# Sums of squares of two head pairs in one batch of four column groups, and the norms' rows issued ahead of the weight loads

## The chip, the cores and the metric

The kernel runs on one core of a Trainium2 chip. The metric is the device time of one execution in microseconds. A profile is one execution of the program, recorded by the hardware profiler.

## The reference, cut to what matters

Four streams of 512 tokens with 256 features go through three layers: a mixture-of-experts feed-forward layer, a state-space layer ("attn" in the names), and the feed-forward layer again. The change is in the state-space layer only:

```
xp, z = x @ Wx.T, x @ Wz.T                       # 512 features = 64 heads x 8
Bm, Cm = (x @ WB.T), (x @ WC.T)                  # each 64 heads x 128 states
Bm = Bm * rsqrt(mean(Bm*Bm, over 128) + 1e-6) * Bn_w + B_bias    # Cm likewise
theta = cumsum((x @ Wth.T) * dt)                 # 64 heads x 64 angles
Bm, Cm = rope(Bm, theta), rope(Cm, theta)
h_t = alpha_t h_(t-1) + beta_t B_(t-1) x_(t-1) + gamma_t B_t x_t;  y_t = C_t . h_t
out = (y * silu(z)) @ Wout.T
```

The norms matter here: for each token and head, the mean of the squares over 128 states of B and of C, then one over its root.

## The kernel before, in words

The state-space layer is done stream by stream: scans 0 to 3, about 1.1 to 2.9 ms into the span. Scans 0 and 1 are unrolled in the program, 2 and 3 are a loop. A scan begins with a preparation (steps dt, decays, values x, which live in all heads) and then runs over 32 pairs of heads. A pair's B and C are four tiles [128, 512]: rows are 2 heads x 64 even (or odd) states, columns are tokens; tiles 0 and 1 are B even and odd, 2 and 3 are C. Four pairs make an iteration of a hardware loop (first and last iteration apart), and each of them is a "turn", even or odd by its place j.

All orders are written out by hand, one function per engine (`turn_pe`, `turn_act`, `turn_pool`, `turn_dve`, `turn_sp`); semaphores tie them. Turn n works on several pairs at once:

- TensorE: the sums of squares of pair n+2 (`ss_pe`, L1220); the outputs y of pair n-2 (`Y_pe`, L1414 and L1416, which waits for the states that `K_dve2` leaves); the products B^T C of pair n-1 (`G_pe`, L1350, which waits for GpSimd's rotation of that pair); transposes (L1359); tiles 0 and 1 of pair n+3 (`A_pe`, whose matmuls all stand at the helper's line L64); the states of pair n-1 (L1390); tiles 2 and 3 of pair n+3; the angles of pair n+2 (`T_pe`, also L64).
- ScalarE evacuates each tile twice: scaled into `xbc` (L1229), squared into `sq4` (L1231). In odd turns it also takes the root of the sums (`R_act`, L1238, into `stdr`, a part of `decay_t`).
- VectorE: angles' scan (`T_dve1`, L1171, waits for `T_pe`), decay scan (L1280), B^T C times the decay (`K_dve1`, L1374, waits for `G_pe`), y out of PSUM in odd turns (L1428, L1432), both norms multiplied in (`F_dve1`, L1274), in odd turns the reciprocal of the next norms (`R_dve`, L1250), four products with sine and cosine (`F_dve3`, L1298), the scan of the states (`K_dve2`, L1399).
- GpSimd: adds the diagonal (L1323), builds it for the next pair (L1318), and adds the products to rotated B and C (`F_pool`, L1306 and L1307); in scans 2 and 3 it also scatters tokens.
- SyncE issues the loads: broadcasts of per-head rows (L1149), angle weights (`th_load_sp`, L1055), the 1 MB of B and C weights for pair n+4 (`wb_load_sp`, L1047), and the norms' way.

The squares of a pair are summed over the partitions by a matmul with a [128, 32] one-hot matrix. f32 matmuls are two passes each, so the four matmuls of a pair are eight instructions in the trace. B goes to partitions 0 to 31 of the bank `SSB` (column group 0 of the array), C to 32 to 63 (group 1); even and odd states accumulate, and so do the two pairs of a couple, each in rows of its own. `sq4` is one buffer: a square of pair m waits for the sums of pair m-1.

After the odd pair of a couple the norms travel: root (`R_act`) -> `R_rows` copies 8 rows x 512 into 128 partitions x 32 (`rc_in`, 16 KB) -> reciprocal (`R_dve`) -> `R_sp2` writes them to memory (L1255) -> `R_sp3` reads them back, broadcast over partitions (`rr_bc`, L1264, 2 x 512 KB). `F_dve1` of the next even turn needs them. In scan 0 `R_rows` is issued by ScalarE's queue, in scans 1 to 3 by SyncE's, behind that turn's loads of `th` and `wb`. Scan 0 also splits each weight into a high and a low part and stores them, which scans 1 to 3 read; ScalarE (L1075, L1089) and VectorE (L1079, L1093) do that.

Of the kernel before, what the change touches and what calls it, by code (L numbers as in the profile page):

```python
# [68 lines left out]
def build(nc, x_in, w_gu, w_down, w_router, w_att, w_x, w_z, w_dtl, w_dth, a_log, w_out, bias_in, norm_w_in,  # L69
          rank_in, ident_in, cst_in, out):  # L70
    with ExitStack() as ctx:
# [88 lines left out]
        rot = [sb(f"rot{i}", [P, 4, SEQ]) for i in range(2)]  # L160
        tmp = sb("tmp", [P, 4, SEQ])
        ths, nfr = (sb(n, [P, SEQ]) for n in ("ths", "nfr"))
        sq4 = sb("sq4", [P, 4, SEQ])
        btr = sb("btr", [P, 2, SEQ])
        x1 = sb("x1", [P, NH, TT, HP])
        rho = sb("rho", [P, NH, TT])
# [17 lines left out]
        neg_a = sb("neg_a", [NH, 1])  # L184
        bias = sb("bias", [P, NP, 4])
        norm_w = sb("norm_w", [P, 4])
        stdr = decay_t[0:36, :, :, :].rearrange("p k q a -> p (k q a)")
        NORM_ROWS = slice(28, 36)
        rc_in, rc = sb("rc_in", [P, 32]), sb("rc", [P, 32])

        dks = [xc[:, i, :] for i in range(2)]
# [15 lines left out]
        oml = tmp[:, 2, TT * NH:].rearrange("p (t n) -> p t n", t=TT)  # L207
        dlt = tmp[:, 3, 0:TT * NH].rearrange("p (t n) -> p t n", t=TT)
        coef = tmp[:, 3, TT * NH:].rearrange("p (t n) -> p t n", t=TT)
        silu_z = [sq4[:, f, :] for f in range(KI)]  # L210
        gated = rot[1]
        row_dram = nc.dram_tensor("row_dram", [NP, 2, ROWW], F32, kind="Internal").ap()
        rr_dram = [nc.dram_tensor(f"rr_dram{i}", [8, SEQ], F32, kind="Internal").ap() for i in range(2)]
# [984 lines left out]
        def A_pe(e, m, j, cnt, parts=range(4), of=by_turns):  # L1198
# [4 lines left out]
            for i in parts:  # L1203
# [4 lines left out]
                else:  # L1208
                    e.wait_ge(e_X.sem, e_X.at(4 * m + i - 1))
                split_matmul(e, of(i)[:, :], [(pair_w(wb[j % 2], i, k), xpair[k]) for k in range(KD)],  # L1210
                             True, True).then_inc(e_pj.sem, 1)

        def ss_pe(e, m, j):
            if j % 2 == 0:
                e.wait_ge(e_sr.sem, e_sr.at(m // 2 if isinstance(m, int) else m >> 1))
            e.wait_ge(e_X.sem, e_X.at(4 * (m + 1)))
            for eo in range(2):
                for ty in range(2):
                    first = 30 - 28 * (1 - ty) - 2 * (j % 2)
                    ins = e.matmul(SSB[32 * ty:32 * ty + 32, :], one_hot[:, first:first + 32], sq4[:, 2 * ty + eo, :],  # L1220
                                   start=j % 2 == 0 and eo == 0, stop=j % 2 == 1 and eo == 1, skip_group_check=True)
            ins.then_inc(e_ssm.sem, 1)

        def A_act(e, m, j, parts=range(4), of=by_turns):
            if parts[0] == 0:
                e.wait_ge(e_t.sem, e_t.at(2 * (m - 3)))
            for i in parts:
                e.wait_ge(e_pj.sem, e_pj.at(4 * m + i + 1))
                e.activation(xbc[j % 4][:, i, :], of(i)[:, :], ACT.Copy, scale=norm_w[:, i:i + 1])  # L1229
                e.wait_ge(e_ssm.sem, e_ssm.at(m))  # L1230
                e.activation(sq4[:, i, :], of(i)[:, :], ACT.Square).then_inc(e_X.sem, 1)  # L1231

        e_rc = ev("e_rc")

        def R_act(e, gm):
            e.wait_ge(e_ssm.sem, e_ssm.at(2 * (gm + 1)))
            e.wait_ge(a_r1.sem, a_r1.at(gm))
            e.activation(stdr, SSB[0:36, :], ACT.Sqrt, scale=1.0 / NS, bias=eps_nm[0:36, 0:1]).then_inc(e_sr.sem, 1)  # L1238

        def R_rows(e, gm):  # L1240
            e.wait_ge(e_sr.sem, e_sr.at(gm + 1))
            e.nop(nofuse=True)
            e.wait_ge(e_rc.sem, e_rc.at(gm))
            e.nop(nofuse=True)
            e.dma_start(rc_in[:, :], stdr[NORM_ROWS, :].rearrange("r (c w) -> r c w", w=32)).then_inc(a_r1.sem, 16)

        def R_dve(e, gm):
            e.wait_ge(a_r1.sem, a_r1.at(gm + 1))
            e.wait_ge(a_r2.sem, a_r2.at(gm))
            e.reciprocal(rc[:, :], rc_in[:, :]).then_inc(e_rc.sem, 1)  # L1250

# [317 lines left out]
        def turn_sp(e, b, it, first, last):  # L1569

            N, Q, NB = b * NP + it * UN, it * UN, NP // UN
            for j in range(UN):
                n, q, p, jp = N + j, Q + j, N + j - 1, (j - 1) % UN
                T, A, SS, RG, K = in_turn(j, first, last)
                gm = b * (NP // 2) + it * 2 + j // 2
                if is_first(b) and not last:
                    wb_load_sp(e, b, q + 4, j)
                if not (last and j >= 2):
                    e.wait_ge(e_tu.sem, e_tu.at(n + 1))
                    e.nop(nofuse=True)  # L1580
                    dt_sp(e, q + 2, j + 2)
                    e.wait_ge(e_H.sem, e_H.at(n - 1))
                    e.nop(nofuse=True)
                    end_sp(e, q + 2, j + 2)
                if not (last and j >= 1):
                    e.wait_ge(e_th.sem, e_th.at(n + 2))
                    e.nop(nofuse=True)
                    th_load_sp(e, b, q + 3, j + 1)
                if not last:
                    e.wait_ge(e_pj.sem, e_pj.at(4 * (n + 3)))  # L1590
                    e.nop(nofuse=True)
                    if not is_first(b):
                        wb_load_sp(e, b, q + 4, j)
                if RG and not is_first(b):
                    R_rows(e, gm + 1)
                if not (last and j >= 2):
                    e.wait_ge(e_D.sem, e_D.at(n + 1))
                    e.nop(nofuse=True)
                    al_sp(e, q + 2, j + 2)
                if RG:  # L1600
                    R_sp2(e, gm + 1, (j // 2 + 1) % 2)
                    R_sp3(e, gm + 1, (j // 2 + 1) % 2)
# [99 lines left out]
            ins.then_inc(e_z.sem, 1)  # L1702

        def z_act(e, b, f):
            e.wait_ge(e_ssm.sem, e_ssm.at((b + 1) * NP))
            e.wait_ge(e_z.sem, e_z.at(KI * b + f + 1))
            e.activation(silu_z[f], XBANK[1][:, :], ACT.Silu).then_inc(e_sz.sem, 1)

# [220 lines left out]
```

## Time and profile before

| | |
|---|---|
| median of 3 runs | 3395.3 us (3392.41 to 3405.55) |
| the profiled execution | 3382.4 us, span 3380.6 us |
| busy: TensorE matmul / weight load | 2799.0 / 2118.0 us (83% / 63%) |
| busy: VectorE / ScalarE / GpSimd | 2326.1 / 1816.0 / 1501.2 us (69% / 54% / 44%) |
| TensorE's granted clock, mean | 0.909 of 2.4 GHz |
| pairs of scan 0 / 1 / 2 / 3, about | 620 to 1140 / 1240 to 1700 / 1850 to 2310 / 2400 to 2860 us |

PE is the matmul side of TensorE and PEld its weight loads, which overlap; DVE is VectorE, ACT ScalarE, POOL GpSimd, SP SyncE; a trailing q is an engine's DMA queue. An idle time in brackets stands before the instruction, with what ended it. Names are those of the program, without buffer numbers, and a view a tile is part of may lend it another name: `stdr` appears as `decay_t`, `SSB` as `bank`.

### The profile page before, as it was taken

To read this page: it belongs to the slowest core of one execution; us is meant where nothing else is said; L and a number is where in the kernel's file an instruction comes from. 1 tells how busy PE (TensorE), PEld (TensorE's weight loads), DVE (VectorE), ACT (ScalarE), POOL (GpSimd) and SP (SyncE) were. 2 spreads that over 40 slices of the span, in tenths; PEclk is the share of its full clock that TensorE was granted. 3 is DMA by queue.
4 is the path that set the end of the run, shared out by engine and by line. 5 is a ranking of instruction groups with operands and counts; after the bars stand their busy time and mean duration, and the time that the engine had idled before them with its cause. 6 is when DMAs were issued, how large, how long until landed. Compare 5 with 4: busy or idle time off the path is not lost.

```text
span 3380.6 us, 83925 instructions
## 1 busy us (share of the span) xinstructions
PE 2799.0 (83%) x28752; PEld 2118.0 (63%) x28752; DVE 2326.1 (69%) x3926; ACT 1816.0 (54%) x3740; POOL 1501.2 (44%) x1354
## 2 busy tenths in 40 slices
PE   4229997789999789999977999998899998549990
PEld 3118885466666557777754677776577776438870
DVE  5205354789999479999855999994799997324364
ACT  1006654577777167666514777763677774126650
POOL 2470155344444344455500666662456665340256
PEclk7559998899999799999978999999999999669995
DMA  9737896556665255566404666652566662548893
GB/s 389 239 131 233 261 296 200 169 181 198 209 192 179 91 158 156 166 172 173 114 1 127 184 175 169 177 152 63 173 179 182 178 174 77 216 138 256 281 288 118
DMA packets 315367, 609.71 MB, mean 180 GB/s; under 512 B 59152, under 2 KB 163728, under 8 KB 314128
## 3 DMA queue, kind: packets, MB, share of 16 engines
q1 hardware_dynamic: 272352, 501.29, 49.3%
q0 software_dynamic: 24576, 67.14, 6.2%
q10 hardware_dynamic: 18224, 38.54, 3.0%
q8 instruction: 120, 1.97, 0.2%
q14 instruction: 95, 0.78, 0.1%
HBM read 446.25 MB, written 159.51 MB: 179 GB/s over the span
## 4 chain that ended last, share of the span: by engine, by line
PE 63%; DVE 8%; ACT 7%; issue 7%; another core or an unknown queue 6%; DMA 5%; POOL 2%; ACTq 1%; SPq 1%; DVEq 0%; POOLq 0%
PE bank L64 23%; PE bank L572 6%; PE bank L1220 6%; PE bank L1350 4%; PE bank L1414 3%; PE bank L1390 3%; PE bank L1416 3%; PE bank L563 2%; PE cs_sn L586 2%; ACT btr L1365 2%; PE bank L1359 2%; PE bank L586 2%; DMA xl<-xd 1%; ACT sq L1231 1%
## 5 line engine op out<-in xcount | busy, mean ns | idle before, releaser
L64 PE MATMUL bank<-xh,wb 128*128 128x512 f32 x2048 | 677.7, 412 | 71.4 <-ACT btr L1365 37.8
L64 PEld LDWEIGHTS bank<-xh,wb 128*128 128x128 f32 x2048 | 367.6, 189 | 188.6 <-ACT btr L1365 58.1
L1229 ACT ACTIVATE xbc<-bank,norm_w 128x512 f32<-128x512 f32 x512 | 350.7, 685 | 234.0 <-PE bank L64 227.5
L1306 POOL TENSOR_TENSOR rot<-rot,tmp 128x512 f32<-128x512 f32 x256 | 330.7, 1292 | 204.0 <-DVE tmp L1298 204.0
L64 PE MATMUL bank<-xl,wb 128*128 128x512 f32 x1024 | 406.6, 397 | 0.0
L572 PE MATMUL bank<-wgu,xgT 128*128 (+1 forms) x1536 | 327.2, 337 | 92.0 <-issue 71.9
L648 DVE TENSOR_TENSOR hh<-sg,bank 128x96 f32<-128x96 f32 x384 | 97.5, 254 | 408.7 <-ACT sg L622 212.8
L1318 POOL TENSOR_TENSOR sq<-cst,rho 128x512 f32<-128x512 f32 x128 | 133.6, 1044 | 494.7 <-DVE xbc L1274 275.1
L1307 POOL TENSOR_TENSOR rot<-rot,tmp 128x512 f32<-128x512 f32 x256 | 331.4, 1295 | 0.0
L1298 DVE SCALAR_TENSOR_TENSOR rot<-xbc,bias,cs_sn 128x1024 f32<-128x1024 f32 x256 | 325.4, 1271 | 8.6 <-DVE xbc L1274 6.8
L1298 DVE SCALAR_TENSOR_TENSOR tmp<-xbc,bias,cs_sn 128x1024 f32<-128x1024 f32 x256 | 326.1, 1274 | 0.0
L1323 POOL TENSOR_TENSOR xc<-xc,sq 128x512 f32<-128x512 f32 x128 | 163.4, 1276 | 358.0 <-DVE xwp L1285 354.6
L1274 DVE TENSOR_TENSOR xbc<-xbc,rr_bc 128x1024 f32<-128x1024 f32 x256 | 308.0, 1244 | 5.7 <-DMA rr_bc<-rr_dram 3.7
L572 PEld LDWEIGHTS bank<-wgu,xgT 128*128 128x128 f32 x1536 | 249.2, 196 | 97.3 <-issue 96.2
L1231 ACT ACTIVATE sq<-bank 128x512 f32<-128x512 f32 x512 | 303.8, 593 | 4.1 <-PE bank L1220 3.1
L1220 PE MATMUL bank<-sq,cst 128*32 128x512 f32 x1024 | 245.3, 600 | 31.8 <-ACT sq L1231 31.0
L1365 ACT ACTIVATE btr<-bank 128x512 f32<-128x512 f32 x256 | 140.3, 595 | 232.5 <-PE bank L1359 230.5
L1416 PE MATMUL bank<-st,rot 128*64 128x16 f32 x3584 | 243.5, 214 | 0.0
L1416 PEld LDWEIGHTS bank<-st,rot 128*64 128x64 f32 x3584 | 230.9, 144 | 0.0
L64 PEld LDWEIGHTS bank<-xl,wb 128*128 128x128 f32 x1024 | 193.7, 189 | 47.9
L1414 PEld LDWEIGHTS bank<-x1p,sq 128*64 128x64 f32 x2048 | 135.5, 143 | 134.8 <-issue 116.7
L616 ACT ACTIVATE xgT<-bank 128x256 f32<-128x256 f32 x384 | 145.8, 380 | 120.2 <-remote 44.2
(293 smaller groups left out, 5840.3 us busy)
## 6 DMA issues: line engine op xcount, KB each, us to landing
wb<-watt_dram SPq DMA_DIRECT2D x96, 1024.0 KB
rr_bc<-rr_dram SPq DMA_DIRECT2D x128, 512.0 KB, 6.5
yd<-ys SPq DMA_DIRECT2D x96, 512.0 KB
wd<-w_down SPq DMA_DIRECT2D x384, 96.0 KB
dt_bc<-row_dram SPq DMA_DIRECT2D x256, 128.0 KB
al_bc<-row_dram SPq DMA_DIRECT2D x256, 128.0 KB
watt_dram<-wb ACTq DMA_DIRECT2D x29, 1024.0 KB, 5.2
xd<-xg SPq DMA_DIRECT2D x12, 2048.0 KB, 23.8
```

The source lines that it names most:

```text
L64: ins = e.matmul(dst, a, m, start=start and c == 0, stop=stop and c == n - 1, skip_group_check=not (start and stop))
L572: ins = e.matmul(gub[n % 2][:, 0:NI2], xgT[n % 3][:, k, :], w, start=k == 0, stop=k == KD - 1)
L1220: ins = e.matmul(SSB[32 * ty:32 * ty + 32, :], one_hot[:, first:first + 32], sq4[:, 2 * ty + eo, :], start=j % 2 == 0 and eo == 0, stop=j ...
L1229: e.activation(xbc[j % 4][:, i, :], of(i)[:, :], ACT.Copy, scale=norm_w[:, i:i + 1])
L1231: e.activation(sq4[:, i, :], of(i)[:, :], ACT.Square).then_inc(e_X.sem, 1)
L1274: e.tensor_tensor(both, both, r.unsqueeze(1).to_broadcast([P, 2, SEQ]), ALU.mult).then_inc(dst.sem, 1)
L1298: ins = e.scalar_tensor_tensor(o[:, 2 * ty:2 * ty + 2, :], X[:, i, :].unsqueeze(1).to_broadcast([P, 2, SEQ]), bias_of(i), cs_sn[:, :, :], ...
L1306: e.tensor_tensor(R[:, 2 * ty, :], R[:, 2 * ty, :], tmp[:, 2 * ty + 1, :], ALU.subtract)
L1307: ins = e.tensor_tensor(R[:, 2 * ty + 1, :], R[:, 2 * ty + 1, :], tmp[:, 2 * ty, :], ALU.add)
L1365: e.activation(btr[:, eo, :], XBANK[x][:, :], ACT.Copy).then_inc(e_bt.sem, 1)
L1414: e.matmul(o, m1[:, (a * TT + t) * CL:(a * TT + t + 1) * CL], c4(x1p[j][:, :])[:, a * TT + t], start=True, stop=True)
L1416: ins = e.matmul(y[CL:P, k, w:w + PW].rearrange("p (a d) -> p a d", a=2), R[:, 2 + eo, CL * k:CL * k + CL], hist[:, eo, :, :, k], start=eo ...
```

## The change

The sums of squares of a couple are taken together in its odd turn. In even turns `ss_pe` only waits for the squares. In odd turns it issues eight matmuls (16 passes): for even, then odd states, one to each of four column groups: B of the even pair, B of the odd pair, C of the even pair, C of the odd pair, at partitions 0, 32, 64 and 96 of the bank. `sq4` becomes two buffers, one per parity. `stdr` becomes a tile of its own with 128 partitions, and `R_rows` two DMAs of 8 KB in place of one of 16 KB. In scans 1 to 3 `R_rows` moves ahead of the `th` and `wb` loads in SyncE's order. Counts of semaphores follow.

```diff
@@ -160,7 +160,8 @@
         rot = [sb(f"rot{i}", [P, 4, SEQ]) for i in range(2)]
         tmp = sb("tmp", [P, 4, SEQ])
         ths, nfr = (sb(n, [P, SEQ]) for n in ("ths", "nfr"))
-        sq4 = sb("sq4", [P, 4, SEQ])
+        sq4 = [sb(f"sq4_{i}", [P, 4, SEQ]) for i in range(2)]
+        stdr = sb("stdr", [P, SEQ])
         btr = sb("btr", [P, 2, SEQ])
         x1 = sb("x1", [P, NH, TT, HP])
         rho = sb("rho", [P, NH, TT])
@@ -184,8 +185,6 @@
         neg_a = sb("neg_a", [NH, 1])
         bias = sb("bias", [P, NP, 4])
         norm_w = sb("norm_w", [P, 4])
-        stdr = decay_t[0:36, :, :, :].rearrange("p k q a -> p (k q a)")
-        NORM_ROWS = slice(28, 36)
         rc_in, rc = sb("rc_in", [P, 32]), sb("rc", [P, 32])
 
         dks = [xc[:, i, :] for i in range(2)]
@@ -207,7 +206,7 @@
         oml = tmp[:, 2, TT * NH:].rearrange("p (t n) -> p t n", t=TT)
         dlt = tmp[:, 3, 0:TT * NH].rearrange("p (t n) -> p t n", t=TT)
         coef = tmp[:, 3, TT * NH:].rearrange("p (t n) -> p t n", t=TT)
-        silu_z = [sq4[:, f, :] for f in range(KI)]
+        silu_z = [sq4[0][:, f, :] for f in range(KI)]
         gated = rot[1]
         row_dram = nc.dram_tensor("row_dram", [NP, 2, ROWW], F32, kind="Internal").ap()
         rr_dram = [nc.dram_tensor(f"rr_dram{i}", [8, SEQ], F32, kind="Internal").ap() for i in range(2)]
@@ -1210,15 +1209,19 @@
                 split_matmul(e, of(i)[:, :], [(pair_w(wb[j % 2], i, k), xpair[k]) for k in range(KD)],
                              True, True).then_inc(e_pj.sem, 1)
 
+        half = lambda m: m // 2 if isinstance(m, int) else m >> 1
+
         def ss_pe(e, m, j):
+            e.wait_ge(e_X.sem, e_X.at(4 * (m + 1)))
             if j % 2 == 0:
-                e.wait_ge(e_sr.sem, e_sr.at(m // 2 if isinstance(m, int) else m >> 1))
-            e.wait_ge(e_X.sem, e_X.at(4 * (m + 1)))
+                e.nop(nofuse=True)
+                return
+            e.wait_ge(e_sr.sem, e_sr.at(half(m)))
             for eo in range(2):
-                for ty in range(2):
-                    first = 30 - 28 * (1 - ty) - 2 * (j % 2)
-                    ins = e.matmul(SSB[32 * ty:32 * ty + 32, :], one_hot[:, first:first + 32], sq4[:, 2 * ty + eo, :],
-                                   start=j % 2 == 0 and eo == 0, stop=j % 2 == 1 and eo == 1, skip_group_check=True)
+                for g in range(4):
+                    first = 30 * (g % 2)
+                    ins = e.matmul(SSB[32 * g:32 * g + 32, :], one_hot[:, first:first + 32], sq4[g % 2][:, 2 * (g // 2) + eo, :],
+                                   start=eo == 0, stop=eo == 1, skip_group_check=True)
             ins.then_inc(e_ssm.sem, 1)
 
         def A_act(e, m, j, parts=range(4), of=by_turns):
@@ -1227,25 +1230,26 @@
             for i in parts:
                 e.wait_ge(e_pj.sem, e_pj.at(4 * m + i + 1))
                 e.activation(xbc[j % 4][:, i, :], of(i)[:, :], ACT.Copy, scale=norm_w[:, i:i + 1])
-                e.wait_ge(e_ssm.sem, e_ssm.at(m))
-                e.activation(sq4[:, i, :], of(i)[:, :], ACT.Square).then_inc(e_X.sem, 1)
+                e.wait_ge(e_ssm.sem, e_ssm.at(half(m)))
+                e.activation(sq4[j % 2][:, i, :], of(i)[:, :], ACT.Square).then_inc(e_X.sem, 1)
 
         e_rc = ev("e_rc")
 
         def R_act(e, gm):
-            e.wait_ge(e_ssm.sem, e_ssm.at(2 * (gm + 1)))
-            e.wait_ge(a_r1.sem, a_r1.at(gm))
-            e.activation(stdr, SSB[0:36, :], ACT.Sqrt, scale=1.0 / NS, bias=eps_nm[0:36, 0:1]).then_inc(e_sr.sem, 1)
+            e.wait_ge(e_ssm.sem, e_ssm.at(gm + 1))
+            e.wait_ge(a_r1.sem, a_r1.at(2 * gm))
+            e.activation(stdr[:, :], SSB[:, :], ACT.Sqrt, scale=1.0 / NS, bias=eps_nm[:, 0:1]).then_inc(e_sr.sem, 1)
 
         def R_rows(e, gm):
             e.wait_ge(e_sr.sem, e_sr.at(gm + 1))
             e.nop(nofuse=True)
             e.wait_ge(e_rc.sem, e_rc.at(gm))
             e.nop(nofuse=True)
-            e.dma_start(rc_in[:, :], stdr[NORM_ROWS, :].rearrange("r (c w) -> r c w", w=32)).then_inc(a_r1.sem, 16)
+            for h in range(2):
+                e.dma_start(rc_in[CL * h:CL * h + CL, :], stdr[CL * h + 30:CL * h + 34, :].rearrange("r (c w) -> r c w", w=32)).then_inc(a_r1.sem, 16)
 
         def R_dve(e, gm):
-            e.wait_ge(a_r1.sem, a_r1.at(gm + 1))
+            e.wait_ge(a_r1.sem, a_r1.at(2 * (gm + 1)))
             e.wait_ge(a_r2.sem, a_r2.at(gm))
             e.reciprocal(rc[:, :], rc_in[:, :]).then_inc(e_rc.sem, 1)
 
@@ -1582,6 +1586,8 @@
                     e.wait_ge(e_H.sem, e_H.at(n - 1))
                     e.nop(nofuse=True)
                     end_sp(e, q + 2, j + 2)
+                if RG and not is_first(b):
+                    R_rows(e, gm + 1)
                 if not (last and j >= 1):
                     e.wait_ge(e_th.sem, e_th.at(n + 2))
                     e.nop(nofuse=True)
@@ -1591,8 +1597,6 @@
                     e.nop(nofuse=True)
                     if not is_first(b):
                         wb_load_sp(e, b, q + 4, j)
-                if RG and not is_first(b):
-                    R_rows(e, gm + 1)
                 if not (last and j >= 2):
                     e.wait_ge(e_D.sem, e_D.at(n + 1))
                     e.nop(nofuse=True)
@@ -1702,7 +1706,7 @@
             ins.then_inc(e_z.sem, 1)
 
         def z_act(e, b, f):
-            e.wait_ge(e_ssm.sem, e_ssm.at((b + 1) * NP))
+            e.wait_ge(e_ssm.sem, e_ssm.at((b + 1) * (NP // 2)))
             e.wait_ge(e_z.sem, e_z.at(KI * b + f + 1))
             e.activation(silu_z[f], XBANK[1][:, :], ACT.Silu).then_inc(e_sz.sem, 1)
 
```

## Rows read from the trace of the kernel before

**Rows 1.** The page: the span, and the costliest-groups row of the sums of squares.
```profile
span 3380.6 us, 83925 instructions
...
L1220 PE MATMUL bank<-sq,cst 128*32 128x512 f32 x1024 | 245.3, 600 | 31.8 <-ACT sq L1231 31.0
```
**Rows 2.** Busy time in one stretch of scan 1; columns: stretch, length, engines, PE clock, DMA.
```profile
1300.00:1600.00 300.00, 293.60 (x3819) 215.62 (x3817) 274.27 (x349) 210.40 (x375) 152.97 (x125) 1.00 0.60 165
```
**Rows 3.** The chain that ended last, two pairs of scan 1: start, us, what.
```profile
1452.39 1.84 PE bank L1220 x8
...
1455.97 1.09 PE bank L1350 x64
...
1466.84 1.84 PE bank L1220 x8
...
1470.42 1.09 PE bank L1350 x64
...
1481.37 1.84 PE bank L1220 x8
```
**Rows 4.** Timeline of VectorE, the same two pairs: start, us, instruction [idle before].
```profile
1452.56 0.70 DVE L1171 SCALAR_TENSOR_TENSOR bank<-bank,dt_bc 128x512 f32<-128x512 f32 x1 [1.07 <-PE bank L64]
...
1457.13 0.76 DVE L1374 TENSOR_TENSOR sq<-bank,xc 128x256 f32<-128x256 f32 x2 [0.52 <-PE bank L1350]
...
1465.21 1.28 DVE L1298 SCALAR_TENSOR_TENSOR tmp<-xbc,bias,cs_sn 128x1024 f32<-128x1024 f32 x1
...
1472.27 2.35 DVE L1274 TENSOR_TENSOR xbc<-xbc,rr_bc 128x1024 f32<-128x1024 f32 x2
...
1479.55 0.84 DVE L1399 TENSOR_TENSOR_SCAN st<-end_bc,bank 64x128 f32<-64x128 f32 x2
1481.54 0.70 DVE L1171 SCALAR_TENSOR_TENSOR bank<-bank,dt_bc 128x512 f32<-128x512 f32 x1 [1.15 <-PE bank L64]
```
**Rows 5.** Timeline of GpSimd: its last rotation of the odd turn's pair.
```profile
1467.94 1.27 POOL L1307 TENSOR_TENSOR rot<-rot,tmp 128x512 f32<-128x512 f32 x1
```
**Rows 6.** Timeline of SyncE's DMA queue, same turn: weight load, norm rows, their way back.
```profile
1454.04 0.57 SPq L1047 DMA_DIRECT2D wb<-watt_dram  x1
1457.36 0.69 SPq L1245 DMA_DIRECT2D rc_in<-decay_t  x1
...
1461.79 0.33 SPq L1255 DMA_DIRECT2D rr_dram<-rc  x1
1463.42 1.29 SPq L1264 DMA_DIRECT2D rr_bc<-rr_dram  x2
```
**Rows 7.** The waits of the whole span: waiter, releaser, us in total, times, longest.
```profile
DVE rc L1250 <- DMA rc_in<-decay_t: 23.3, 29, 1.9
```
**Rows 8.** Timeline of SyncE's DMA queue, an odd turn of scan 2: the weight load.
```profile
2094.77 0.57 SPq L1047 DMA_DIRECT2D wb<-watt_dram  x1
```
**Rows 9.** Timeline of VectorE in that turn: the reciprocal of the norm rows.
```profile
2103.07 0.35 DVE L1250 RECIPROCAL rc<-rc_in 128x32 f32<-128x32 f32 x1 [1.66 <-DMA rc_in<-decay_t]
```
**Rows 10.** DMA issues of 1300 to 1600 us: the last number is us to landing.
```profile
rr_bc<-rr_dram SPq DMA_DIRECT2D x20, 512.0 KB, 5.8
```
**Rows 11.** Timeline of VectorE in scan 0, two pairs.
```profile
899.41 0.70 DVE L1171 SCALAR_TENSOR_TENSOR bank<-bank,dt_bc 128x512 f32<-128x512 f32 x1 [1.10 <-PE bank L64]
...
904.85 0.74 DVE L1374 TENSOR_TENSOR sq<-bank,xc 128x256 f32<-128x256 f32 x2
...
928.63 0.84 DVE L1399 TENSOR_TENSOR_SCAN st<-end_bc,bank 64x128 f32<-64x128 f32 x2
930.48 0.70 DVE L1171 SCALAR_TENSOR_TENSOR bank<-bank,dt_bc 128x512 f32<-128x512 f32 x1 [1.01 <-PE bank L64]
```
**Rows 12.** Timeline of TensorE, the same two pairs of scan 0.
```profile
902.97 1.16 PE L1350 MATMUL bank<-rot 64*64 64x64 f32 x64
...
915.79 1.91 PE L1220 MATMUL bank<-sq,cst 128*32 128x512 f32 x8 [1.57 <-ACT sq L1231]
```
**Rows 13.** Timeline of ScalarE's DMA queue in scan 0: the norm rows' issue.
```profile
904.22 0.69 ACTq L1245 DMA_DIRECT2D rc_in<-decay_t  x1
```

## The prediction

> **What bounds the kernel now.** First the busy table by stretch. In scan 1 between 1300 and 1600 us TensorE is busy 293.60 of 300 us at full granted clock (2.4 GHz), VectorE 274.27, ScalarE 210.40, GpSimd 152.97 [rows 2]. TensorE is the bound, VectorE close behind. Then the chain of waits: over two pairs it runs through TensorE's own instructions, with ScalarE's evacuation of the transposes (0.6 us a turn) the only other engine on it. A couple of pairs, from one odd turn's sums of squares to the next, takes 1481.37 - 1452.39 = 28.98 us [rows 3]. The two blocks of sums stand on that chain with 1.84 us each. Last the timelines of VectorE and GpSimd, for what is late next. VectorE waits 1.15 us for the angles' matmuls at the start of an odd turn, 0.52 us for the B^T C products in the middle of it [rows 4], and in some odd turns for the norms' rows: 23.3 us in 29 waits, 1.9 us at most [rows 7].
>
> **Part 1, the even turn's sums go.** TensorE loses 1.84 us per couple [rows 3]. The wait for the squares stays and costs no more than now, as the next instruction but one (`Y_pe`) needs the state scan of the odd turn anyway.
>
> **Part 2, the odd turn's sums double.** 16 passes in four column groups in place of 8 in two. Of today's 8 passes each takes 600 ns [rows 1], yet the 8 take 1.84 us: two run abreast, 0.46 us a round. If four run abreast, 16 passes are again four rounds, 1.84 us; if only two, 3.7 us. Those are the bounds (nothing speaks for less than 1.84). The nearest row is L1350: 64 passes of 64 columns, an eighth of the columns, so 0.058 us a round; two abreast they would take 1.8 us, four abreast 0.93 us plus one pass's tail. They take 1.09 [rows 3]. Its tiles are two row halves by two column halves, and not four column groups, but four different streams do enter the array at once. I take 1.84 us.
>
> Against it stands a rule: the Trainium skill, "TensorE: Matmul & The Clock Gate", section "Part 3: Packing small matmuls — row/col tiling", measured three column groups of 32 at 2.38 times one, not 3. By that efficiency the block would take about 2.3 us, an estimate from that page, and each couple would lose 0.5 us of the gain worked out below; no row here has more than two column groups of 32 at work.
>
> **What is late next in scans 1 to 3.** If TensorE alone counted, a couple would take 27.1 us. But the even turn's G_pe (L1350, 1470.42) would then start at 1468.6, and it needs the rotated pair, whose last GpSimd operation ends at 1467.94 + 1.27 = 1469.21 [rows 5]. So G_pe moves up to about 1469.3 only. The ring that closes is: G_pe even to sums odd, 1481.37 - 1470.42 = 10.95; sums odd to G_pe odd, 1455.97 - 1452.39 = 3.58; to VectorE's product that waits for it, 1457.13 - 1455.97 = 1.16 [rows 3, 4]; from there to the end of its last rotation product, 1465.21 + 1.28 - 1457.13 = 9.36 [rows 4]; to the end of GpSimd's last addition, 1469.21 - 1466.49 = 2.72; and 0.1 to wake TensorE. Sum 27.87 us, 1.1 less than 28.98. VectorE by itself needs 1479.55 + 0.84 - 1452.56 = 27.83 with its waits for TensorE in it, 27.3 without the 0.52, so it fits under this ring.
>
> This ring holds only in turns in which the reciprocal does not wait for the norms' rows; today that wait hides behind TensorE, in the new ring it would stand on the path at its full size (23.3 us over 48 couples, 0.5 each).
>
> **Part 3, the rows go ahead of the weight load.** The rows are issued when the root is there (1457.36), after the loads of `th` and `wb` (1454.04) [rows 6]. They arrive behind the 1 MB: in the slowest turns 8.3 us after the weight load's issue (2094.77 to 2103.07, with 1.66 us of wait) [rows 8, 9]. Ahead of the loads they meet an empty queue, and the wait goes. That gives back the 0.5 us a couple.
>
> But something is queued behind them now. `th` and `wb` are held until the root is there. With the rows' second DMA (another 0.3 to 0.7 us of issue, from the 0.33 and 0.69 of rows 6) the weight load leaves some 2.2 us after the rows, at about 1459.6 instead of 1454.04. Its own user, the next turn's first projection, is at about 1472, so the load is in time. The reciprocals, however, are sent off at 1461.79 as today, and now it is they that stand behind 1 MB. Bounds: if they pass the weights, they land as today, at 1463.4 [rows 6]; if they wait as the rows do in the slowest turn, at 1459.6 + 8.3 + 0.5 (for the decay rows between them) = 1468.4. I take 6.6 us behind the weight load's issue, since the nearest transfer of the same size, the two halves of `rr_bc`, needs 0.65 + 5.8 = 6.5 [rows 6, 10]: 1466.7. Then `rr_bc` is issued and lands 6.5 us later, at 1473.2 (bounds 1469.9 and 1474.9). VectorE wants it at 1472.27 [rows 4].
>
> Is that 0.9 us on the path? In the new order VectorE has the 0.52 us wait before its product in the odd turn to swallow part of it. The ring through the norms spans two couples: sums odd to rows 5.0 (1452.39 to 1457.36), rows to `rr_bc` 15.8, even norm product to next angle scan 8.2 (1472.27 to 1480.47), angle scan to last rotation product 13.93 - 0.52 = 13.4, GpSimd and wake 2.8, G_pe to sums 10.95 [rows 3 to 6]. Sum 56.2, or 28.1 us a couple. It is longer than 27.87 by 0.25, and every further microsecond of landing costs 0.5. With the bounds of the landing a couple takes 27.9 to 28.95 us. I take 28.1: 0.88 us less than today. A scan has 15 even turns with sums (one more is in the preparation), so 3 x 15 x 0.88 = 39.6 us, less 2 for first and last turns: 38.
>
> The Trainium skill, "DMA: Bandwidth & Descriptors", section "Queues, rings and completion order", says that the descriptors of an issuing engine are taken in ring order on each DMA engine, but that completion is not first in, first out: a small transfer may finish on some rings early. If it let the 16 KB pass the weights, `rr_bc` would be in time and the sum 45 x 1.1 = 50 us for scans 1 to 3. The trace is against it: 16 KB wait for 1 MB today [rows 7].
>
> **Part 4, scan 0.** The order of DMAs stays. Two pairs take 930.48 - 899.41 = 31.07 us. VectorE is busy without a pause longer than 0.2 us from 899.41 to 928.63 + 0.84 = 929.47, then waits 1.01 [rows 11]; TensorE waits 1.57 us for squares before the even turn's sums [rows 12]. Without the sums G_pe of the even turn starts 1.84 us earlier, and VectorE's wait goes: 30.07 us a couple, 1.0 less, times 15 is 15 us. The second small DMA sits in ScalarE's queue there (0.69 us for the one now [rows 13]), just before the evacuation of the transposes; its 0.35 to 0.7 us fit into the 0.8 us by which TensorE is then ahead. If that cover were gone it would cost up to 0.7 x 15 = 10 us.
>
> **Part 5, at nothing.** The preparation loses one block of sums per scan and one wait of the squares; its steps run on VectorE and SyncE, so 0, at most 4 x 1.84 = 7 us gained. The root over 128 instead of 36 partitions, the buffers and the counts: 0.
>
> **Sum.** 38 + 15 = 53 us off the profiled execution's own 3382.4: 3329.4. The median of the runs stands 12.9 above that execution, so 3342.
>
> **Rivals.**
> A. The norms come late for good. If the reciprocals land 8.4 us or more behind the weight load's issue in place of 6.6, the ring is 28.98 and beyond: scans 1 to 3 gain nothing, and lose 45 x 0.5 = 22 us per further microsecond. For it: the load is held 5.5 us, and the longest wait today stands for 8.3 us; against it: in most turns the wait is far under that. At the edge 3395 - 15 = 3380; slower than before from 9.1 us on (the 15 us of scan 0 are then spent), and at 10.5 us about 3412. Chance 0.14, of which 0.04 ends slower.
> B. The four groups do not run abreast. The odd block takes 3.7 us, TensorE saves nothing, and the block stands in the ring of scans 1 to 3 (it lies between angles and G_pe, for which VectorE waits): 28.1 + 1.84 = 29.9, 0.95 more than today, 45 times 43 us. In scan 0 G_pe ends at 904.13 and VectorE comes at 904.85 [rows 11, 12], so 1.1 us of wait eat the gain there. 3395 + 43 = 3438. It decides from a block longer than about 2.8 us. Against it: L1350. Chance 0.07.
> C. All of it comes, and more: the norms in time, VectorE's slack found, a couple at 27.4 to 27.5 us, the preparation's share too: 45 x 1.55 + 15 + 5 = 90 us, 3305. VectorE's 27.3 allow it; the ring through GpSimd speaks against it. Chance 0.15.
> D. The move does nothing (the rows still wait 0.5 us): 28.4 us, 26 + 15 = 41 us, 3354; within the forecast's range.
>
> **How the numbers follow.** The forecast has 0.60, range 3325 to 3362; A 0.14, B 0.07, C 0.15, and 0.04 is for what I don't see. The overall range is 3308 to 3384. What a measurement of this kernel can tell is 0.5%, 17 us. Faster by more: forecast, C, and 0.05 of A: 0.80. Within: 0.09 of the rest of A and others: 0.11. Slower: B and the end of A: 0.09.
>
> **What would show it.** Right: L1220 only in odd turns, 16 passes in about 1.9 us; a couple in scans 1 to 3 at 27.9 to 28.3 us; no more wait of L1250 for `rc_in`; a wait of up to 1 us of L1274 (even turns) for `rr_bc`; TensorE waiting under 1 us before the even turn's outputs or L1350; scan 0 at 30.1 us with no wait of L1171. Wrong: a block of 2.5 us or more (B), waits of L1274 above 2 us (A), a granted clock below full in the middle of the scans, or a couple under 27.6 us (C).

## The result, and the profile after

The changed kernel takes 3500.91 us (median of 3, 3493.09 to 3506.56), the kernel before 3395.3. The ratio is 1.0301, 95% interval 1.0255 to 1.0348: 106 us slower, where 53 us faster had been forecast. The profiled execution has a span of 3491.3 us.

The page after has a new wait in the row of VectorE's norm product, 5.7 us in all before (3.7 of them for `rr_bc`). Columns as in [rows 1].

```profile
L1278 DVE TENSOR_TENSOR xbc<-xbc,rr_bc 128x1024 f32<-128x1024 f32 x256 | 306.0, 1237 | 159.3 <-DMA rr_bc<-rr_dram 140.3
```

VectorE now stands idle 140.3 us for `rr_bc` ahead of that product. The busy table by stretch (engines in the order PE, PEld, DVE, ACT, POOL, then granted clock, DMA share, GB/s): three pieces of one couple of scan 0, and 300 us of scan 1, which answers to [rows 2].

```profile
918.00:930.60 12.60, 9.56 (x86) 7.30 (x84) 12.29 (x18) 9.63 (x18) 7.02 (x6) 1.00 0.68 223
930.60:937.40 6.80, 6.80 (x107) 6.31 (x105) 5.59 (x9) 2.58 (x5) 1.27 (x1) 0.50 0.94 245
937.40:950.00 12.60, 12.37 (x169) 8.94 (x172) 10.45 (x12) 10.20 (x18) 6.10 (x5) 1.00 0.33 123
1350.00:1650.00 300.00, 273.69 (x3551) 212.78 (x3549) 256.20 (x330) 197.34 (x348) 142.15 (x117) 0.94 0.54 154
```

TensorE is no longer the bound (273.69 of 300 where it was 293.60), and the clock, which was granted in full in these pairs before, falls to 1.2 GHz at times, in scan 0 twelve times in twelve couples. The second row is such a fall. TensorE's timeline there: it waits for the squares of the even turn, and the outputs (`Y_pe`, 16 columns each) come right behind.

```profile
930.10 0.20 PE L1418 MATMUL bank<-x1p,sq 128*64 128x16 f32 x1 [2.08 <-ACT sq L1234]
```

The 64 passes of `G_pe` behind them took 1.99 us, where they had taken 1.16 in [rows 12].

A couple in scan 1, TensorE's timeline: the sums are in odd turns only, 16 passes in 1.92 us, as forecast. Eight passes over two groups had taken 1.91 us in such a timeline [rows 12], which the chain of [rows 3] has as 1.84.

```profile
1508.20 1.92 PE L1223 MATMUL bank<-sq,cst 128*32 128x512 f32 x16
```

VectorE over the same couple answers to [rows 4]: angle scan of the odd turn, the reciprocal, the even turn's norm product with its wait, and the next odd turn's angle scan.

```profile
1479.93 0.70 DVE L1170 SCALAR_TENSOR_TENSOR bank<-bank,dt_bc 128x512 f32<-128x512 f32 x1
...
1489.22 0.34 DVE L1254 RECIPROCAL rc<-rc_in 128x32 f32<-128x32 f32 x1
...
1503.31 2.36 DVE L1278 TENSOR_TENSOR xbc<-xbc,rr_bc 128x1024 f32<-128x1024 f32 x2 [3.03 <-DMA rr_bc<-rr_dram]
...
1511.47 0.70 DVE L1170 SCALAR_TENSOR_TENSOR bank<-bank,dt_bc 128x512 f32<-128x512 f32 x1
```

SyncE's queue answers to [rows 6]: rows, angle weights, the 1 MB, decay rows, reciprocals, `rr_bc`.

```profile
1484.73 1.29 SPq L1249 DMA_DIRECT2D rc_in<-stdr  x2
1486.35 0.62 SPq L1054 DMA_DIRECT2D th<-watt_dram  x1
1487.31 0.60 SPq L1046 DMA_DIRECT2D wb<-watt_dram  x1
1488.14 1.21 SPq L1148 DMA_DIRECT2D al_bc<-row_dram  x2
1489.63 1.20 SPq L1259 DMA_DIRECT2D rr_dram<-rc  x1
1495.92 1.29 SPq L1268 DMA_DIRECT2D rr_bc<-rr_dram  x2
```

And ScalarE, in the odd turn: the rounding of the angles, which waits for VectorE's scan, and the root directly behind it.

```profile
1481.92 0.69 ACT L1184 ACTIVATE bank<-cum,magic 128x512 f32<-128x512 f32 x1 [1.53 <-DVE cum L1173]
1482.63 1.28 ACT L1241 ACT_TABLE_LOAD   x1
1483.92 0.69 ACT L1241 ACTIVATE stdr<-bank,eps_nm 128x512 f32<-128x512 f32 x1
```

Read together they show a ring that closes in one couple: VectorE's angle scan (1479.93), rounding, root, rows issued (1484.73, 4.8 us later); weights, reciprocals, `rr_bc`, norm product (1503.31, 18.6 us later); angle scan of the next couple (1511.47, 8.2 us later). Sum 31.5 us. It is no single case: over 42 couples of scans 1 to 3 the medians are 4.8, 18.4 and 8.2 us, and a couple has a median of 31.4. The 1 MB left at 1487.31, and the reciprocals behind it had landed only when `rr_bc` could be issued, 8.6 us later. From their own issue (1489.63) that is 6.3 us, where it was 1.6 before the change [rows 6]. `rr_bc` itself then took 7.4 us where 6.5 had been usual.

### The profile page after: what moved, and what is told of

The parts are those of the page before. It is cut to its first block, busy times and chain, and to the rows that moved or that the text cites. A ratio compares the mean times of both kernels' runs of the same rounds, so it can differ in the third digit from the quotient of the medians.

```text
span 3491.3 us, 84063 instructions
## 1 busy us (share of the span) xinstructions
PE 2790.0 (80%) x28752; PEld 2189.7 (63%) x28752; DVE 2319.1 (66%) x3926; ACT 1821.7 (52%) x3740; POOL 1471.3 (42%) x1354
## 4 chain that ended last, share of the span: by engine, by line
PE 31%; DMA 17%; DVE 16%; issue 11%; ACT 8%; another core or an unknown queue 6%; SPq 5%; POOL 3%; ACTq 2%; DVEq 1%; POOLq 0%
DMA rr_bc<-rr_dram 7%; DMA rr_dram<-rc 6%; PE bank L571 6%; PE bank L64 5%; DVE tmp L1302 3%; DVE xbc L1278 3%; PE bank L562 2%; PE bank L1354 2%; PE cs_sn L585 2%; PE bank L585 2%; DVE rot L1302 2%; ACT L1241 2%; PE bank L1420 1%; ACT sq L1234 1%
## 5 line engine op out<-in xcount | busy, mean ns | idle before, releaser
L64 PE MATMUL bank<-xh,wb 128*128 128x512 f32 x2048 | 690.7, 419 | 79.2 <-ACT btr L1369 39.2
L64 PEld LDWEIGHTS bank<-xh,wb 128*128 128x128 f32 x2048 | 375.7, 194 | 194.8 <-ACT btr L1369 59.3
L1278 DVE TENSOR_TENSOR xbc<-xbc,rr_bc 128x1024 f32<-128x1024 f32 x256 | 306.0, 1237 | 159.3 <-DMA rr_bc<-rr_dram 140.3
L1418 PE MATMUL bank<-x1p,sq 128*64 128x16 f32 x2048 | 151.5, 216 | 143.5 <-DVE st L1403 112.9
L1420 PE MATMUL bank<-st,rot 128*64 128x16 f32 x3584 | 259.1, 219 | 0.0
L1420 PEld LDWEIGHTS bank<-st,rot 128*64 128x64 f32 x3584 | 246.3, 152 | 0.0
L1354 PE MATMUL bank<-rot 64*64 64x64 f32 x8192 | 192.3, 259 | 25.1 <-POOL rot L1311 22.0
```

The costliest lines, as they stand in the source:

```text
L64: ins = e.matmul(dst, a, m, start=start and c == 0, stop=stop and c == n - 1, skip_group_check=not (start and stop))
L1278: e.tensor_tensor(both, both, r.unsqueeze(1).to_broadcast([P, 2, SEQ]), ALU.mult).then_inc(dst.sem, 1)
L1354: ins = e.matmul(o, R[h, eo, CL * k:CL * k + CL], R[h, 2 + eo, CL * k:CL * k + CL], start=eo == 0, stop=eo == 1)
L1418: e.matmul(o, m1[:, (a * TT + t) * CL:(a * TT + t + 1) * CL], c4(x1p[j][:, :])[:, a * TT + t], start=True, stop=True)
L1420: ins = e.matmul(y[CL:P, k, w:w + PW].rearrange("p (a d) -> p a d", a=2), R[:, 2 + eo, CL * k:CL * k + CL], hist[:, eo, :, :, k], start=eo ...
```

## The experiments

"Couple" below is the mean over 12 couples of a scan, from the start of `G_pe`'s products in its fourth turn to those in its twenty-eighth; scans 1 to 3 are averaged. The clock column counts the stretches at 1.2 GHz inside those 12 couples, scan 0 / scans 1 to 3 together. Couples and falls are those of the one profiled execution of each kernel. Ratios are to the kernel before on the same chip. Experiments 1 to 4 ran on one chip (kernel before 3389.14 us), 5 to 8 on a second (3266.44 us; the part ahead of scan 0's pairs alone is some 70 us shorter), 9 to 11 on a third (3392.77 us), so only ratios go from one group to another.

| kernel | ratio (95%) | scan 0 | scans 1-3 | falls |
|---|---|---|---|---|
| before | 1 | 31.4 | 29.0 | 0 / 0 |
| changed | 1.0301 (1.0255-1.0348) | 32.5 | 31.4 | 12 / 29 |
| 1 rows back | 1.0066 (1.0042-1.0089) | 32.1 | 29.6 | 12 / 17 |
| 2 move only | 1.0182 (1.0156-1.0207) | 31.2 | 30.7 | 0 / 9 |
| 3 two DMAs | 1.0034 (1.0020-1.0048) | 32.0 | 29.3 | 0 / 0 |
| 4 rows back, filled | 1.0137 (1.0070-1.0204) | 30.7 | 30.3 | 3 / 17 |
| 5 rows back, wb first | 0.9970 (0.9955-0.9986) | 32.1 | 28.5 | 11 / 11 |
| 6 before, wb first | 0.9987 (0.9976-0.9999) | 31.3 | 28.9 | 0 / 0 |
| 7 as 5, filled | 1.0033 (1.0008-1.0058) | 32.6 | 29.2 | 3 / 6 |
| 8 loads last | 1.0450 (1.0425-1.0474) | 32.2 | 32.3 | 11 / 43 |
| 9 as 5, wait later | 0.9931 (0.9913-0.9948) | 30.7 | 28.7 | 2 / 13 |
| 10 changed, root first | 1.0092 (1.0070-1.0115) | 31.6 | 29.6 | 10 / 15 |
| 11 changed, filled | 1.0295 (1.0264-1.0327) | 32.3 | 32.0 | 4 / 28 |

**1. Rows put back behind the loads.**

```diff
-                if RG and not is_first(b):
-                    R_rows(e, gm + 1)
                 if not (last and j >= 1):      # th load, then wb load
 ...
+                if RG and not is_first(b):
+                    R_rows(e, gm + 1)
                 if not (last and j >= 2):      # al load
```

> The changed kernel with R_rows put back behind the th and wb loads; the batched sums stay. Theory Q (the norms' way through the DMA queue sets the couple in scans 1 to 3): the waits of L1278 for rr_bc go, scans 1 to 3 fall from 31.4 us a couple to 27.9 to 28.5, so 3370 to 3390. Theory C (TensorE's granted clock falls in the even turn, now without its dense block, and that is the cost): scan 0 stays at 32.0 us a couple, since nothing changes there; in scans 1 to 3 the clock still falls about once a couple and a couple takes 29.5 to 30.5, so 3440 to 3480. If C were all, the time would stay at 3500.

Measured: 3412.4 us, three quarters of the loss gone. No wait for `rr_bc` is left in scan 1; scan 0 is nearly as slow as in the changed kernel (32.1 and 32.5). Both theories hold in part: the order of DMAs is the larger piece, and the batch is slower than before even without it. It landed between the two forecasts, with 17 falls of the clock in scans 1 to 3, and with the reciprocal waiting for its rows again (10.0 us in 6 waits from 1330 to 1680 us).

**2. Only the move, in the kernel before.** The inverse of the edit above, in the kernel before.

> The kernel before with R_rows moved ahead of the loads in scans 1 to 3 and nothing else. Theory Q: the ring is root to rr_bc 17.9 us (one DMA of rows in place of two saves 0.7 of the 18.6 measured), rr_bc to the next angle scan 8.2, angle scan to root and rows 4.8: 30.9 us a couple in place of 28.98, 45 times, so 3480; scan 0 as before. Theory C: the dense block stays in every turn, the clock stays full, 3395.

Measured: 3453.32 us, less than the 3480 of the ring, but a couple at 30.7 us is close to its 30.9. VectorE's waits from 1340 to 1680 us of this kernel (waiter, releaser, us, times, longest):

```profile
DVE xbc L1274 <- DMA rr_bc<-rr_dram: 33.0, 10, 4.4
```

The move alone costs 62 us (1.82%). Nothing of the batch is needed for it. The clock falls 9 times in scans 1 to 3 although the even turn's sums are still there.

**3. Two DMAs for the rows, in the kernel before.**

```diff
-            e.dma_start(rc_in[:, :], stdr[NORM_ROWS, :]...)
+            for h in range(2):
+                e.dma_start(rc_in[CL * h:CL * h + CL, :], stdr[28 + 4 * h:32 + 4 * h, :]...)
```

> The kernel before with R_rows as two DMAs of four rows each, in the old place of the order. Both theories: the issue takes 0.6 us longer. In scans 1 to 3 the wait of the reciprocal grows by up to 0.6 us and still hides behind TensorE, 0 to +10 us in all. In scan 0 the issue stands in ScalarE's queue before the evacuation of the transposes: up to 0.6 us a couple, 0 to +9 us. So 3395 to 3415. A rival in which the second DMA carries much of the loss would give 3440 or more.

Measured: 3401.64 us against 3389.14, 12 us more. As expected: 0.6 us a couple in scan 0 (on ScalarE's queue), 0.3 in the others. The Trainium skill, "DMA: Bandwidth & Descriptors", section "Rules for kernel authors", says not to split a transfer into two partition halves; here the split costs 0.34%.

**4. Rows back, and unread matmuls in the even turns.**

```diff
-        def ss_pe(e, m, j):
+        def ss_pe(e, m, j, fill=0):
+            if j % 2 == 0 and fill:
+                e.wait_ge(e_sr.sem, e_sr.at(half(m)))
+                unread(e, SSB[:, :], fill)
             e.wait_ge(e_X.sem, e_X.at(4 * (m + 1)))
...
-                    ss_pe(e, n + 2, j)
+                    ss_pe(e, n + 2, j, 6 if is_first(b) else 3)
```

> As the first kernel (rows back behind the loads), with matmuls whose result nobody reads at the start of the even turn, ahead of its wait for squares: 6 in scan 0, 3 in scans 1 to 3 (0.24 us each). Theory C: the granted clock stays full, scan 0 falls from 32.0 to 30.1 to 30.6 us a couple, scans 1 to 3 to 28.0 to 28.5; 3345 to 3375. If only Q counts the filler does nothing or costs up to 0.7 us a couple: as the first kernel or up to 30 us above it.

Measured: 3423.53 us, a miss in the total. Scan 0 takes 30.7 us a couple instead of 32.1 (30.1 to 30.6 had been expected), with 3 falls of the clock instead of 12. With TensorE kept at work through its wait for squares the loss of scan 0 turns into a gain of 0.7 us a couple on the kernel before. In scans 1 to 3 only one couple of the 36 takes 27.97 us (between the sums at 2119.51 and those at 2147.48), near the 27.87 of the forecast's ring through GpSimd. Most take 29 to 31, with 17 falls of the clock as in 1 and waits of the reciprocal for its rows. Two take about 37, with TensorE idle for a reason that the profile calls "issue".

**5. As 1, with the 1 MB load moved up.**

```diff
+                if not last and not is_first(b):
+                    e.wait_ge(e_pj.sem, e_pj.at(4 * (n + 3)))
+                    e.nop(nofuse=True)
+                    wb_load_sp(e, b, q + 4, j)
                 if not (last and j >= 2):
                     e.wait_ge(e_H.sem, e_H.at(n - 1))       # then end_bc, th, rows
```

> The batched sums with the rows back behind the loads, and in scans 1 to 3 the wb load moved up: ahead of the wait for the state scan and the end_bc load, so that it leaves as soon as its buffer is free, some 4 us earlier. Theory: what is left of the loss in scans 1 to 3 of the first kernel (29.6 us a couple) is the reciprocal's wait for rows behind the 1 MB, which makes TensorE wait for the state scan, which drops its clock. Then L1254 no longer waits, low-clock stretches in the middle of scans 1 to 3 go, and a couple takes 27.9 to 28.2; scan 0 keeps its 32.1. Time: 3412 - 45 x 1.5 = 3345. Rival: the clock falls for want of the even turn's dense block alone; then low-clock stretches stay and a couple takes 29.3 or more, 3400.

Measured: 3255.42 us against 3266.44, faster than before. The reciprocal waits no more; scans 1 to 3 take 28.5 us, 0.4 under the same chip's kernel before with the same move (6). Between the two forecasts again: couples without a fall take 27.9 to 28.0 once a scan has run in, and about one in three takes 1.2 us more, where the clock falls. Its timeline in such a place, the products of three turns:

```profile
1484.91 1.16 PE L1354 MATMUL bank<-rot 64*64 64x64 f32 x64
...
1498.38 1.84 PE L1354 MATMUL bank<-rot 64*64 64x64 f32 x64 [0.25 <-POOL rot L1311]
```

The same 64 passes take 1.84 us instead of 1.16.

**6. The kernel before with that load moved up.** The edit of 5 alone.

> The kernel before with the same wb load moved up and nothing else. The reciprocal's waits (23.3 us in all) go, but TensorE stays the bound at 28.98 a couple: 3380 to 3392, no change that can be told. Rival: the waits were on the path before too; then up to 23 us go, 3366.

Measured: ratio 0.9987, some 4 us, where the waits of [rows 7] are 23 in all. They were for the most part hidden behind TensorE.

**7. Both: load moved up and filler.** Edits 4 and 5.

> Batched sums, rows behind the loads, wb load moved up, and the unread matmuls in even turns (6 in scan 0, 3 in the others). Scan 0 as with the filler before, 30.7 us a couple; scans 1 to 3 at 27.9 to 28.2, as in the undisturbed couples of the filled kernel (27.97). Time 3389 - 10 - 45 x 1.0 = 3330 to 3340. If the filler costs more in scans 1 to 3 than the clock does, it comes out above the kernel without it by up to 30 us less the 20 of scan 0.

Measured: 3278.72 us, a miss. The clock falls 9 times instead of 22, and undisturbed couples take 27.96 to 28.08, as eleven of the twelve of scan 2 do, without a fall among them; but five turns of scans 0 and 1 take 20 us or more, where 14 to 16 is usual. Such a place, TensorE's timeline:

```profile
1344.75 0.26 PE L1421 MATMUL bank<-x1p,sq 128*64 128x16 f32 x1 [3.92 <-issue]
```

TensorE stands idle there while every engine that it could wait for is done. In the pairs of the kernels without the filler no such wait is longer than 1.7 us. Why three or six more matmuls bring them is open.

**8. Rows ahead, both loads behind the whole way of the norms.** `th` and `wb` loads go behind `R_sp3` in odd turns.

> The changed kernel, rows ahead, but in odd turns of scans 1 to 3 the th and wb loads go behind the whole way of the norms (behind the reads of rr_bc). Theory Q, that the 16 KB of reciprocals stood behind the 1 MB: rr_bc is issued 6 to 6.5 us after the rows as in the kernel before, its wait in L1278 goes. The weights leave 5 to 6 us later still and queue behind rr_bc's 1 MB, so TensorE's first projection of the even turn may wait up to 3 us for them: a couple 28 to 30.5, 3380 to 3460. If the wait for rr_bc came from something else (the two DMAs of rows, the batch), it stays at about 4 us and the time at 3500.

Measured: 3417.05 against 3266.44. The wait for `rr_bc` is gone from scan 1, which shows that it came from the weights in front of the reciprocals (the 1 MB and the 256 KB of `th`, which moved together here). In its place TensorE waits for the weights (1330 to 1680 us). A couple takes 32.3 us where 28 to 30.5 had been expected, a miss:

```profile
PE bank L64 <- DMA wb<-watt_dram: 21.4, 9, 4.7
```

**9. As 5, with the even turn's wait for squares behind `Y_pe` and `G_pe`.**

```diff
-                if SS:
+                if SS and j % 2:
                     ss_pe(e, n + 2, j)
...
                     G_pe(e, p, jp)
+                if SS and j % 2 == 0:
+                    ss_pe(e, n + 2, j)
+                if K:
                     tr_pe(e, p, jp, 0, 0)
```

> Batched sums, rows behind the loads, wb load moved up, no filler; and the even turn's wait for the squares stands behind the outputs and the B^T C products (Y_pe, G_pe) instead of ahead of them, where the transposes need it. In scan 0 TensorE waited 2.1 us there. Theory C: without that idle stretch the clock falls less often in scan 0, and Y_pe and G_pe no longer run at half clock: scan 0 from 32.1 to 30.1 to 30.8 us a couple; scans 1 to 3 as without the change, 28.0 to 28.5. Against the kernel before: -20 in scan 0, -25 in the others, ratio 0.985 to 0.992. Rival: the thin matmuls of Y_pe and G_pe don't keep the clock whatever stands before them; then scan 0 stays near 32 and the ratio near 0.997.

Measured: 3371.26 against 3392.77, ratio 0.9931, just short of the 0.985 to 0.992 expected, and the best of all here. Scans 1 to 3 take 28.7 us, where 28.0 to 28.5 had been expected. Scan 0 takes 30.7 us a couple with 2 falls of the clock instead of 11, without one added matmul. Both falls are in its first two couples (33.6 and 33.8 us, with waits for squares of about 4 us); eight of the other ten take 29.9 to 30.1, the 30.07 of the forecast, where the kernel before takes 31.1 to 31.2. Moving the wait also lets outputs and products run before it, so this run alone doesn't separate that from the clock; experiment 4 leaves the wait where it is. This kernel keeps the batch, drops the move and orders load and wait anew.

**10. The changed kernel with ScalarE's root ahead of its rounding.**

```diff
-                if T:
-                    T_act2(e, n + 1, j + 1)
                 if RG:
                     R_act(e, gm + 1)
+                if T:
+                    T_act2(e, n + 1, j + 1)
```

> The changed kernel (rows ahead of the loads, as changed) with one swap on ScalarE in odd turns: the root of the sums ahead of the rounding of the angles (L1184), which waits for VectorE's scan. Theory: in scans 1 to 3 the ring is next angle scan, rounding, root, rows, weights, reciprocals, rr_bc, norm product, angle scan, 31.4 us in one couple. The root then needs only TensorE's sums, which are done 3 us before the scan: rows leave 2 to 4 us earlier against VectorE, the wait for rr_bc falls by as much, a couple falls to 28.5 to 30, 45 x 2 = 90 us off, ratio to the kernel before 1.000 to 1.010 in place of 1.030. Rival (as in the prediction): the norms' way starts from TensorE's sums anyway and takes two couples to close; then the swap moves nothing, 1.03.

Measured: 3425.43 against 3392.77, ratio 1.0092 where the changed kernel has 1.0301. A couple falls by 1.7 us to 29.6, without a change to any DMA's order. ScalarE's timeline in an odd turn of it, the root now first:

```profile
1501.55 0.69 ACT L1241 ACTIVATE stdr<-bank,eps_nm 128x512 f32<-128x512 f32 x1
1502.13 0.69 ACT L1184 ACTIVATE bank<-cum,magic 128x512 f32<-128x512 f32 x1
```

The rows leave at 1502.44, 3.7 us after that turn's angle scan (1498.77) instead of 4.8; in most turns it is less. The medians over 42 couples of scans 1 to 3, here and in the changed kernel: angle scan to rows 2.65 and 4.81 us; rows to norm product 18.7 and 18.4; norm product to the next angle scan 8.2 in both. Their sums are 29.5 and 31.4, the median couples 29.7 and 31.4. So the rounding, and VectorE's scan before it, are links of the ring, and the ring closes in one couple. The reciprocals are issued 3.5 us behind the weight load here and 2.2 in the changed kernel, yet land 8.75 and 8.4 us behind it: their landing goes by the weight load.

**11. The changed kernel with the filler alone.** Edit 4 without edit 1.

> The changed kernel as it is, with the unread matmuls in even turns (6 in scan 0, 3 in scans 1 to 3) and nothing else. Clock theory: scan 0 falls from 32.4 to about 30.7 us a couple, 15 x 1.7 = 25 us off. Ring theory: scans 1 to 3 stay at 31.0 to 31.4, as the wait for rr_bc sets them whatever the clock. Ratio to the kernel before 1.022 to 1.026. If the clock were the larger part, 1.010 or less.

Measured: ratio 1.0295 where 1.022 to 1.026 had been expected, a miss, and no gain. Scans 2 and 3 stay at 31.5 us, as the ring says. Scan 1 takes 33.1, with three couples of about 40. Scan 0 has 4 falls instead of 12 but two turns of 22 us with the long "issue" waits, which eat the gain. In scans 1 to 3 the clock still falls 28 times, against 29, so this run can't tell what it costs there; that the ring sets these scans is shown by 2 and 10.

## Why the prediction was wrong

- **Four groups abreast: right.** 16 passes took 1.92 us, and rival B fell. The Trainium skill, "TensorE: Matmul & The Clock Gate", section "Part 3: Packing small matmuls — row/col tiling", has three column groups at 2.38 times one, by which the prediction had estimated 2.3 us; the trace doesn't agree with that for four.
- **The ring through GpSimd, 27.87 us: right as a bound.** Kernels 5, 7 and 9 (and one couple of 4) reach 27.9 to 28.1 in couples with nothing else in the way. VectorE is near its own limit there too (280.56 of 300 us busy in a stretch of 5), and no run tells the two apart.
- **The wait of the reciprocal goes with the move: right**, and worth little, since today TensorE hides it (6). In the batched kernel it costs more than the 0.5 us a couple that was set down for it: loading the weights earlier takes a couple from 29.6 to 28.5 us (1 against 5, on two chips), with 11 falls of the clock for 17.
- **The ring through the norms, 28.1 us: the step that failed.** It said "sums odd to rows 5.0", as if the rows left by TensorE's clock, and spread one late landing over two couples at 0.5 us each. The 5.0 us are in truth VectorE's angle scan to rows, 4.8 us: the root stands behind the rounding, which waits for that scan, as a view of ScalarE before the change shows, in the turn of [rows 4]:

```profile
1454.55 0.69 ACT L1185 ACTIVATE bank<-cum,magic 128x512 f32<-128x512 f32 x1 [0.73 <-DVE cum L1174]
...
1456.55 0.68 ACT L1238 ACTIVATE decay_t<-bank,eps_nm 36x512 f32<-36x512 f32 x1
```

  So the ring closes in one couple, and a late landing counts in full. With the forecast's own sizes it gives 4.8 + 15.8 + 8.2 = 28.8 us and no gain to speak of in scans 1 to 3. The two-couple ring with the landing as measured (2.8 us more, next item) gives 29.5 us, still 1.9 short of the couple. Experiment 10 shows the link.
- **The landing, second term of that ring: mis-sized.** Weight load issue to reciprocals landed was 8.6 us, forecast 7.1; `rr_bc` 7.4, forecast 6.5; the rest is issue. That makes rows to norm product 18.6 us instead of 15.8. The bound of 8.3 + 0.5 had covered it; the middle value was taken from `rr_bc`'s own size, and not from the slowest turn, though that was the nearer case (16 KB behind the same 1 MB). The ring with measured terms is 31.5 us, the couple 31.4.
- **Rival A was the one that came**, with the right place and half the slope: 22 us per microsecond where the one-couple ring makes it 45. Its figure at 10.5 us was also wrong in the adding: by its own terms about 3426, not 3412.
- **The clock: not among the steps at all.** The text expected full clock and named its loss only as a sign of error. The even turn's sums were counted as 1.84 us of load to be rid of, but they were also what TensorE did right after its wait for squares. Without them a wait of up to 2.1 us is followed by `Y_pe`'s 16-column matmuls, and the clock falls to 1.2 GHz: the second row of the table by stretch. There the products of a turn take 1.99 us instead of 1.16, and scan 0 takes 32.1 us a couple in 1 and 32.5 in the changed kernel, where it took 31.4 and 30.1 had been forecast. Experiments 4 and 9 show it by two different edits, 12 falls to 3 and 11 to 2, with scan 0 at 30.7, and at 29.9 to 30.1 in the undisturbed couples of 9. So the forecast's term for scan 0 was right but for the clock. That activity gives the clock back and its lack takes it is what the Trainium skill says in "TensorE: Matmul & The Clock Gate", section "Part 1: The HAM clock gate (the "warmup" mystery)"; the trace agrees (0.50 from 930.6 to 937.4 us, 1.00 on either side).
- **The second DMA: within its bounds, not at nothing.** 12 us (3), forecast 0 with up to 10 in scan 0 if uncovered. In the kernel before it is uncovered, 0.6 us a couple of scan 0; experiment 9 has the second DMA and reaches the forecast's 30.1 with it, so the cover can hold.

The sum of the parts: the move alone costs 62 us (2), and the changed kernel without it 22 us (1), 12 of which are the second DMA's in the kernel before (3). That makes 84 of the 102 us that the changed kernel's ratio stands for. The intervals of the three ratios together leave the other 18 uncertain by some 20, so it isn't shown that the two parts cost more together than apart. The clock falls more often with both (29 times in scans 1 to 3, against 17 and 9), but what that costs there was not measured.

## What to carry to other kernels

When a stage's time is set by a ring, walk it on every engine that it crosses, in the engine's own order, before a number is put on its slope: one instruction that stands in front of another on a queue (here a rounding in front of a root) can close in one iteration a ring that seemed to span two. A small transfer moved ahead of a large one saves its own wait and hands that wait to the small transfer that follows, so move the large one away from both. Work taken off TensorE can cost its clock; see what is left between the wait and the next dense matmuls.

## What was not expected of the hardware

- A DMA issue can itself take longer: `rr_dram<-rc` took 1.20 us close behind the 1 MB, 0.33 us before [rows 6]. From 1350 to 1650 us its median is 1.25 us in the changed kernel and 0.33 in 10, where it follows the same 1 MB 3.5 us later instead of 2.2. The cause stays open.
- 16 passes over four column groups of 32 took 1.92 us, as 8 passes over two had (1.91 us [rows 12]).
- The granted clock fell in scan 0 after waits of at most 2.1 us, when thin matmuls followed. Waits of up to 1.8 us for the same squares, with the dense sums behind them, left it full before the change (waits from 700 to 1080 us of the kernel before):

```profile
PE bank L1220 <- ACT sq L1231: 20.1, 14, 1.8
```

- A few unread matmuls brought "issue" waits of up to 6.1 us on TensorE in all three kernels that had them (4, 7, 11). The cause stays open.
